# The first batch of a two-layer cross-attention kernel: key stores ahead of the row loads, statistics and later key work one pair earlier

## The reference, cut to what matters

```python
# layer 0
q, k, v = x @ Wq + bq, ctx @ Wk + bk, ctx @ Wv + bv          # 32 query heads, 8 key/value heads
attn = softmax(q k^T * 16**-0.5 + mask)
x = layernorm((attn v) @ Wo + bo + x) * gamma + beta
# layer 1
a = layernorm(ctx) * ln_gamma + ln_beta
Q, K, V = x @ Wq.T, a @ Wk.T, a @ Wv.T                       # 16 heads of width 32
attn = softmax(where(mask, Q K^T * 32**-0.5, -inf))
out = x + tanh(gate) * ((attn V) @ Wo.T)
```

## Time and profile before

| | us |
|---|---|
| median of 3 executions | 1139.96 |
| lowest, highest | 1139.66, 1144.16 |
| the profiled execution's own time | 1139.66 |
| its span in the profile | 1137.9 |
| PE busy in the span | 1111.0 (98%) |
| DVE, ACT, POOL busy | 803.7, 762.8, 246.1 |

### The profile page before, as it was taken

The page is one execution under the profiler, slowest core; times in us unless marked ns, Lnnn a source line. Parts: engine busy times, 40 slices in busy tenths (PEclk is TensorE's granted clock), DMA queues, the critical chain, the costliest instruction groups (busy, mean ns, idle before and its releaser), DMA issues.

```text
span 1137.9 us, 28561 instructions
## 1 busy us (share of the span) xinstructions
PE 1111.0 (98%) x9963; PEld 941.0 (83%) x9963; DVE 803.7 (71%) x2609; ACT 762.8 (67%) x2325; POOL 246.1 (22%) x263
## 2 busy tenths in 40 slices
PE   8899999999999999999999999999999999999998
PEld 6778888888878888888888878888788888878877
DVE  4755858767685876858767685876858767685865
ACT  4656848577584866848578484866848578584865
POOL 1332123131121312122131221312123131221310
PEclk9999999999999999999999999999999999999999
DMA  7985745375473745746375464745746375474530
GB/s 242 220 210 119 178 95 160 95 156 154 97 182 91 177 115 119 178 96 160 96 155 154 97 172 105 174 113 117 180 93 163 96 156 153 97 186 97 121 81 9
DMA packets 78620, 155.23 MB, mean 136 GB/s; under 512 B 10587, under 2 KB 47459, under 8 KB 77967
## 3 DMA queue, kind: packets, MB, share of 16 engines
q1 hardware_dynamic: 78350, 152.99, 55.6%
q10 hardware_dynamic: 128, 0.41, 0.2%
HBM read 113.72 MB, written 39.65 MB: 135 GB/s over the span
## 4 chain that ended last, share of the span: by engine, by line
PE 74%; issue 7%; DVE 7%; ACT 7%; DMA 3%; SPq 0%; DVEq 0%; POOL 0%; ACTq 0%
PE PJ L383 19%; PE TP L434 9%; PE SCO L420 7%; PE SCO L707 5%; PE SCO L478 5%; PE OA L454 5%; PE PJ L486 5%; PE SCO L434 5%; ACT PR L1090 5%; PE PJ L396 4%; DVE PR L848 3%; PE SCO L383 3%; PE OA L459 2%; PE SCO L424 2%; DVE TH L801 1%
## 5 line engine op out<-in xcount | busy, mean ns | idle before, releaser
L1090 ACT ACTIVATE PR<-PR,MN 100x361 f32<-100x361 f32 x768 | 451.2, 591 | 87.2 <-DVE MN L848 83.7
L848 DVE CUSTOM_DVE_ANT_0 PR<-SCO,MK 100x361 f32<-100x361 f32 x768 | 383.8, 529 | 116.0 <-PE SCO L420 76.0
L434 PE MATMUL TP<-ident,PR 100*128 100x100 f32 x1536 | 196.6, 250 | 3.9 <-ACT PT L1101 2.5
L434 PEld LDWEIGHTS TP<-ident,PR 100*128 100x128 f32 x1536 | 167.1, 141 | 29.8 <-ACT PR L1090 4.2
L420 PE MATMUL SCO<-K0S,Q0S 128*100 128x362 f32 x512 | 156.0, 371 | 3.9 <-DVE MN L848 1.4
L1090 ACT ACTIVATION_READ_ACCUMULATOR PR<-PR,MN 100x1 f32 x768 | 145.6, 190 | 0.0
L860 DVE COPY PT<-TP 121x300 f32<-121x300 f32 x256 | 119.0, 465 | 23.8 <-PE TP L434 22.4
L1101 ACT ACTIVATE PT<-TP 121x300 f32<-121x300 f32 x256 | 103.4, 404 | 18.1 <-PE TP L434 17.9
L434 PE MATMUL SCO<-ident,PR 100*128 100x100 f32 x768 | 110.1, 252 | 3.7 <-ACT PT L1101 3.6
L1290 POOL TENSOR_TENSOR K1F<-K1F,KB 128x364 f32<-128x364 f32 x64 | 50.7, 793 | 262.7 <-DVE K1F L841 262.7
L1293 POOL TENSOR_TENSOR K1HL<-K1F,K1HL 128x364 fp32r<-128x364 f32 x64 | 61.9, 967 | 189.4 <-ACT K1HL L1128 189.4
(11 more groups left out here) (150 smaller groups left out, 2015.5 us busy)
## 6 DMA issues: line engine op xcount, KB each, us to landing
K1S<-k_scr SPq DMA_DIRECT2D x128, 364.0 KB, 6.3
k_scr<-K1HL SPq DMA_DIRECT2D x64, 364.0 KB, 2.8
Q0S<-q_scr SPq DMA_DIRECT2D x124, 100.0 KB, 4.3
K0S<-k_scr SPq DMA_DIRECT2D x64, 182.0 KB, 4.8
AT<-ctx_cols SPq DMA_DIRECT2D x16, 722.0 KB, 10.0
V<-ctx_rows SPq DMA_DIRECT2D x16, 484.0 KB
q_scr<-QHL SPq DMA_DIRECT2D x16, 400.0 KB, 2.5
k_scr<-K1HL SPq DMA_DIRECT2D x32, 182.0 KB, 3.1
```

Source lines behind the costliest of these rows:

```text
L434: last = pe.transpose(turned(k)[:, c * T:(c + 1) * T], PR[0:T, k % NPR, c * SP:c * SP + P], ident[0:T, 0:T])
L848: dve.tensor_tensor_reduce(out=PR[0:T, k % NPR, 0:S], in0=SCO[0:T, k % 2, 0:S], in1=mask[0:T, :], scale=scale, scalar=3.4e38, op0=ALU.add, ...
L1090: act.activation(PR[0:T, k % NPR, 0:S], PR[0:T, k % NPR, 0:S], ACT.Exp, bias=MN[0:T, k:k + 1], scale=-1.0, accum_out=SM[0:T, k:k + 1]).the ...
```

## The change

Everything in it lies in the prologue's end and the first batch. SP: the stores of key blocks 0 and 1 go ahead of the loads of batch 1's context rows, the residual rows `R0` and the constant rows `ROWS`; `ROWS` goes ahead of `XT`; blocks 2 and 3 are stored, and half 0 of the keys loaded back, ahead of the load of `WQ1`. PE: the six unread matmuls and the wait ahead of them go; key steps 24 to 47 follow pairs 5 to 8 in place of 6 to 9; `rstd_rows` goes ahead of the transposes of its pair. DVE: the statistics of batch 0's context move from pairs 2 and 3 to 1 and 2; the four scalings stay at pairs 5, 7, 9, 11, but ahead of the pair's two shifts in place of behind them. ACT: `rstd_out` moves from pair 5 to 4.

```diff
-        FIRST_K1_STEPS = spans({-1: 12, 0: 2, 1: 3, 2: 3, 3: 2, 4: 2, 6: 6, 7: 6, 8: 6, 9: 6})
+        FIRST_K1_STEPS = spans({-1: 12, 0: 2, 1: 3, 2: 3, 3: 2, 4: 2, 5: 6, 6: 6, 7: 6, 8: 6})
...
+            store_keys1(0, 0)
+            store_keys1(0, 1)
             sp.wait_ge(c_st, 3)
             load_ctx_rows(1)
             sp.dma_start(R0[0:T, :], x_rows[0]).then_inc(l_xn, 16)
+            sp.dma_start(ROWS[:, :], rows.partition_broadcast(P)).then_inc(l_row, 16)
             sp.wait_ge(q0_mm, 1)
             sp.dma_start(XT, x_cols[1]).then_inc(l_xt, 16)
-            sp.dma_start(ROWS[:, :], rows.partition_broadcast(P)).then_inc(l_row, 16)
-            store_keys1(0, 0)
-            store_keys1(0, 1)
+            store_keys1(0, 2)
+            store_keys1(0, 3)
+            load_keys1(0, 0)
             sp.wait_ge(wk_c, C)
             sp.dma_start(WQ1[:, :, :], wq1).then_inc(l_wq1, 16)
-            load_keys1(0, 0)
-            store_keys1(0, 2)
-            store_keys1(0, 3)
...
                     first_keys1_steps(-1)
-                    pe.wait_ge(q0_l, 4)
-                    repeated_keys(6)
...
+                    elif first and p == 4:
+                        pe.wait_ge(wv_c, C)
+                        rstd_rows(0)
...
-                    if first and p == 4:
-                        pe.wait_ge(wv_c, C)
-                        rstd_rows(0)
...
+                    if first and p in (5, 7, 9, 11):
+                        keys1_scaled(b, (p - 5) // 2)
                     for k in (2 * p, 2 * p + 1):
                         shift(b, k)
-                    if first and p in (5, 7, 9, 11):
-                        keys1_scaled(b, (p - 5) // 2)
-                    elif first and p == 2:
+                    if first and p == 1:
                         ctx_stats(b, 0)
                         ctx_stats(b, 1)
-                    elif first and p == 3:
+                    elif first and p == 2:
                         ctx_stats(b, 2)
                         ctx_mean(b)
...
-                    elif first and p == 5:
+                    elif first and p == 4:
                         act.wait_ge(pad_zero, 2)
                         rstd_out(0)
```

## The result

The changed kernel took 1150.2 us at the median of its executions (1147.1 to 1151.7), the kernel before 1141.2 beside it: a ratio of 1.0073, with a 95% interval of 1.0051 to 1.0093. (The ratio is taken over all executions, so it need not be that of the medians.) A second comparison of the same two gave 1.0053 [1.0033, 1.0073]. So the change makes the kernel slower by 6 to 8 us; the medians differ by 9.0 and 7.1 us. The direction and the place were forecast, the size (+3.5 us, 1143.5) was not.

The account below looks back on a forecast made before the run. PE's work bounds the kernel, with some 6 us of holes up to 61 us; late context rows (+2.5) and low clock (+1.0) make +3.5 us, 1143.5 in median terms; range 1138.5 to 1146.5, the forecast's own 1142 to 1145.

Parts of the forecast that it names:

- The place: PE up to 61 us: a shift in when it gets past that point goes into the time one for one.
- The mechanism: SP's stream: key store lands at 56.0 for 58.9; rows issued 12.7 us later; DVE waits at pair 9, delaying PE.
- The compute engines' edits: Removed matmuls: 0; earlier statistics cost 0.9 us; scalings' 0.8 us given back; block 1's remainder 1 us later, before the clock.
- rival 1: Batch 1, pair 9: ACT's wait goes, nothing follows: -2.4 us, 1137.6; chance 0.18 with its weak form.
- `WQ1` and the other late data: Loads issued later in SP's stream by 10 us or more; `WQ1` keeps 8 us of slack; taken as 0.
- X: Landing of batch 1's context rows: 59.9 us, bounds 57.4 and 61.7, or 62.2 at the latest store; +2.5 us.
- the rows' own term: Batch 1's context rows land 3.9 us behind the store, two thirds of 5.8 us for rows and store.
- its own estimate by engines: Context rows on 11 and 7 DMA engines: 2.8 us, X = 58.8, a sum 1.1 us smaller.
- The clock behind the hole: PE after its idle of over 4 us near 61 us: 1.2 GHz for 3 us, at most 1.5, taken as 1.0 us.
- The sum: Whole kernel: +2.5 + 1.0 = +3.5 us on 1139.66, so 1143.2, or 1143.5 in the median's terms.
- rivals 2 and 4: DVE's slow load plus low clock: +5.8, 1145.8, chance 0.06; later data late: 1148.5 with 5 us late, chance 0.04.
- rival 2: DVE's stall at pair 9 with X = 61.7 and 1.5 us of low clock: +5.8, 1145.8; chance 0.06.

Follow-up runs that it names:

- b1: Kernel before without the six unread matmuls and the wait ahead of them, nothing else; ratio 0.9999 to the kernel before.
- b3: Kernel before with the new order on PE, DVE and ACT alone, SP's order and the six matmuls kept; ratio 1.0008.
- a1: Changed kernel with batch 1's context rows loaded ahead of the two key stores again; 1142.0 us, ratio 0.9993 to the kernel before.
- b4: Kernel before with the two key stores moved behind batch 1's context rows but ahead of `R0`, `XT` and `ROWS`; ratio 0.9993.
- a0: Changed kernel again, nothing altered, for a second profile; 1149.7 us at the median, ratio 1.0053 to the kernel before.
- a2: Changed kernel with the six unread matmuls and the wait ahead of them put back; ratio 1.0067 to the kernel before.
- b2: Kernel before with only SP's new order of issues, the other engines and six matmuls as before; ratio 1.0058.
- a4: Changed kernel with SP waiting for DVE's first statistics of batch 1 before issuing `R0`, `ROWS` and `XT`; ratio 1.0057 to the kernel before.
- c1: Changed kernel with batch 1's context rows loaded in four pieces of 112, 9, 112 and 7 partitions; ratio 1.0051 to the kernel before.
- c2: Changed kernel with batch 1's context rows issued between the two key stores; ratio 1.0013 to the kernel before.
- d2: Changed kernel, rows first, six matmuls back, batch 1's context columns and layer 0's output weights held until batch 0's first statistics; 1139.9 us, ratio 0.9979.
- d3: Kernel before with b4's store order, and batch 1's context columns and layer 0's output weights held until batch 0's first statistics; 1139.8 us, ratio 0.9972.

## Why the prediction was wrong

**Right.** The place: PE ahead of 61 us, and its shift going into the time one for one. The mechanism: the store wins, the rows lose, and DVE at pair 9 carries the loss to ACT and PE. The compute engines' edits near nothing in time (b1, b3). The gain of the store without the price, 2.4 us in rival 1: 1.8 us in the stretch of a1 and 2.3 across the hole in b4, though in neither clear of noise in time. `WQ1` and the other late data cost nothing: PE had no wait behind 63.6 us in this batch beyond 0.2 us. The fall of the clock behind the hole. Block 0 was scaled at 45.18 and block 1 at 49.66, as forecast within 0.2 us. DVE's first wait was 1.88 us and not 2.8, in this profile with a low clock ahead of it; in a0 it was 3.36.

**The term that was mis-sized** is X, the landing of the rows: 59.9 was said, with 62.2 as the latest; DVE was released at 62.40. Of the 2.5 us, 0.5 came from the store's issue (53.7 for 53.2: its data was ready at 52.73 + 0.96), 1.0 from its landing (57.5 for 56.0, less that 0.5), and 1.0 from the rows (4.9 us behind the store, for 3.9). How the last two share it is an accident of this execution; the rows' own term is what failed. Counted from where the store released ACT, DVE got the rows 4.7 us later here, and 6.3, 5.7 and 6.6 in a0, a2 and b2, for the 3.9 of the sum. The 3.9 us had been taken from batch 1, as two thirds of the time of rows and store. The prediction let a queue serve in turn, and shared that time by bytes. It left out what was to be issued behind the rows, and it put its own estimate by engines, which pointed to the uneven pieces, in the direction of a shorter time. a4 and c1 show both costs: with nothing behind the rows, and with even pieces, it is 3.9 us in each (57.86 to 61.79, 57.64 to 61.54).

**The clock behind the hole** was put at 1.0 us. From 63.59 to 67.39 it took 3.80 us where the prediction's steps have 2.6 at the full clock: 1.2 us, right for this execution. In a0 it was about twice that, 2.5 us up to the second score behind the hole. It was taken from one profile of before, and a stretch there had one length.

**The sum.** The first profile gives +6.2 at the marked score and +5.4 in time, for +3.5. It was the fastest of all executions of the changed kernel. a0, near the median, adds 4.2 us: 0.7 from the later end of DVE's wait, 1.3 from the longer low clock, and 2.2 behind batch 1's first score, whose cause stays open. The absolute number had a further fault: it started from three executions with a median of 1139.96, and in the later comparisons, with 17 and 29 executions, the kernel before had medians of 1142.5, 1143.8 and 1141.9. The profiled one was among its fastest, and its profile is one of the few without a low clock before the first score (below).

**The chances.** "Slower by over 0.5%" had 0.07, since it was tied to rivals 2 and 4; rival 2 is the one that came nearest, with X beyond its 61.7 and more low clock.

## What to carry to other kernels

When a store is moved ahead of a load in one issue stream, the load inherits the wait for the store's data. Read for each DMA that is passed over when its first reader asks, and what stands behind that reader on its engine; a load that was issued 13 us before its first reader asked (40.85, 54.20) came 6 us too late once it had been moved. A transfer that someone waits for is best followed by nothing that can wait: here what stood behind a load cost it 1.3 us or more in one place and some 1.4 in another, and only the kernels that also held back what isn't needed beat the kernel before clear of noise. And count with the clock behind a hole in TensorE: holes of 5.3 and 5.9 us cost 6.5 and 8.4 here.

## What the runs showed of the hardware beyond that

The 5 us between executions of one kernel arise in part ahead of everything that was changed. In the profile of b2 the clock stood at 1.2 GHz from about 13.5 to 20.5 us, with PE busy throughout, and the first score came at 35.9 us; in the profile of before the same stretch ran at the full clock, and it came at 32.3. The two, first b2:

```profile
14.00:20.00 6.00, 6.00 (x24) 6.00 (x25) 2.48 (x4) 2.21 (x4) 0.00 (x0) 0.50 0.42 163
```

```profile
14.00:20.00 6.00, 6.00 (x46) 5.66 (x45) 5.12 (x7) 4.88 (x8) 0.00 (x0) 1.00 0.61 204
```

The same instructions, ahead of the first edit. The low clock came there in eleven of the fourteen profiles, and the first score goes with it: 32.1 to 32.7 us in the three without it (before, changed, a0), 33.2 to 34.2 in four with some 3.4 us of it (a4, b1, b3, c1), 35.1 to 36.9 in seven with some 7 us (a1, a2, b2, b4, c2, d2, d3). What the engine did before differs too. Its eight first matmuls, from 4.9 us on, between which the program waits for the four pieces of a weight load, were done later: the next group began at 9.9 to 10.6 us in the first seven profiles and at 10.9 to 11.6 in the seven with the long low stretch. Whether that is the cause, and what made those eight slower, was not tried; the pieces of the load landed 4.0 to 5.1 us after their issue in both groups. From 72 to 1130 us no profile shows the low clock again, yet the time left from batch 1's first score on still differs by 3.4 us between executions.
